# Splitting each expert tile's sixteen matmuls over two steps of the scan loop on TensorE

## What is computed

```python
u, v = split(x @ in_proj_w.T + in_proj_b)
delta = softplus(u @ delta_proj_w.T); A = -exp(a_log)
Bmat = (u @ b_proj_w.T + b_proj_b).reshape(Bsz, L, G, N)
u_conv = silu(causal_conv(u))
# scan over time, for 1024 channels x 16 states:
h = exp(delta * A) * h + (delta * u_conv) * B;  y = sum_n h * c
attn = y * silu(v)

shared_out = swiglu(fx @ w_shared_in) @ w_shared_out
hid = swiglu(fx @ w1_shared)
for e in range(8):
    routed_out += wdense[:, e:e+1] * (hid @ w2[e])      # wdense: top-2 gate weights
```

## Time and profile before

| | us |
|---|---|
| median of two runs | 5194.6 (5162.02 and 5227.19) |
| the profiled execution, its own time | 5190.78 |
| span of its slowest core (core 3), from first to last instruction | 5189.2 |
| spans of the eight cores | 5139.2 to 5189.2 |
| mean granted clock of PE, by core | 0.770 to 0.788 |

### The profile page before, as it was taken

The page is one execution under the profiler, slowest core; times in us unless marked ns, Lnnn a source line. Parts: engine busy times, 40 slices in busy tenths (PEclk is TensorE's granted clock), DMA queues, the critical chain, the costliest instruction groups (busy, mean ns, idle before and its releaser), DMA issues.

```text
span 5189.2 us, 45260 instructions; the slowest of 8 cores (5139.2 to 5189.2 us)
## 1 busy us (share of the span) xinstructions
PE 2806.7 (54%) x10240; PEld 1037.8 (20%) x10240; DVE 3187.6 (61%) x4304; ACT 1671.4 (32%) x2403; POOL 1746.5 (34%) x2319
## 2 busy tenths in 40 slices
PE   0025764556725765457645667258663577455673
PEld 0002221212202221122212222022221222121221
DVE  0014788268863789357872788527884478825886
ACT  0014521353213712255213622137121452225421
POOL 0002544045420634035340544206340264403543
PEclk9997886678857987588866888568775688667885
DMA  9961220212211221112212122012211122121220
GB/s 105 111 96 64 71 92 35 83 48 75 86 42 51 75 75 68 53 55 76 83 35 83 58 75 83 34 51 75 75 68 41 59 75 84 43 77 40 74 85 25
DMA packets 50961, 348.47 MB, mean 67 GB/s; under 512 B 6224, under 2 KB 6480, under 8 KB 16880
## 3 DMA queue, kind: packets, MB, share of 16 engines
q1 hardware_dynamic: 46144, 302.30, 16.7%
q0 software_dynamic: 1488, 34.88, 6.3%
q10 hardware_dynamic: 3072, 8.39, 0.5%
HBM read 363.66 MB, written 51.38 MB: 80 GB/s over the span
## 4 chain that ended last, share of the span: by engine, by line
DVE 30%; PE 25%; issue 16%; POOL 11%; ACT 7%; another core or an unknown queue 7%; DMA 3%; DVEq 1%; POOLq 0%; ACTq 0%; SPq 0%
DVE hsc L816 13%; POOL ysc L847 7%; DVE dBu L811 6%; PE pEG L929 6%; DVE hg L778 4%; DVE uc L718 3%; PE pAB L877 3%; PE pAB L480 3%; PE pFF L480 2%; PE pBCb L594 2%; DVE accb L576 1%; POOL acc L852 1%; POOL state L843 1%; PE pBCb L462 1%
## 5 line engine op out<-in xcount | busy, mean ns | idle before, releaser
L671 ACT ACTIVATE dA<-dlt,A_sb 128x512 f32<-128x512 bf16 x1024 | 737.0, 721 | 1946.9 <-DVE hsc L816 1943.0
L929 PE MATMUL pEG<-hg,ring 128*128 128x512 bf16 x4096 | 1041.2, 413 | 548.9 <-DVE hg L778 390.6
L816 DVE TENSOR_TENSOR_SCAN hsc<-dA,state,dBu 128x512 bf16<-128x512 f32 x768 | 1265.9, 1648 | 82.9 <-DVE dBu L811 3.7
L847 POOL TENSOR_TENSOR ysc<-hsc,ysc 128x512 f32<-128x512 bf16 x960 | 1129.5, 1177 | 0.8 <-issue 0.8
L811 DVE TENSOR_TENSOR dBu<-du,pBCb 128x512 bf16<-128x512 bf16 x1024 | 684.7, 669 | 441.8 <-PE pBCb L948 397.8
L843 POOL CAST state<-hsc 128x1 f32<-128x1 bf16 x1024 | 224.0, 219 | 1707.9 <-DVE hsc L816 1694.5
L929 PEld LDWEIGHTS pEG<-hg,ring 128*128 128x128 bf16 x4096 | 409.1, 104 | 1171.7 <-issue 865.9
L826 POOL TENSOR_TENSOR du<-du,dlt 128x512 bf16<-128x512 bf16 x64 | 73.6, 1149 | 1672.8 <-ACT du L656 1672.8
L948 PE MATMUL pBCb<-b_sb,csel_sb 32*128 32x512 bf16 x1024 | 392.1, 426 | 401.5 <-DVE dBu L811 360.6
L816 DVE TENSOR_TENSOR_SCAN hsc<-dA,dBu 128x512 bf16<-128x512 f32 x256 | 420.5, 1643 | 26.8 <-DVE dBu L811 0.5
L462 PE MATMUL pBCb<-ident,xnp 128*128 128x128 f32 x256 | 94.6, 446 | 581.8 <-DVE xnp L422 558.3
(11 more groups left out here) (94 smaller groups left out, 2980.4 us busy)
## 6 DMA issues: line engine op xcount, KB each, us to landing
ring<-wsbf SPq DMA_DIRECT2D x256, 1024.0 KB, 4.8
wsbf<-wstream POOLq DMA_DIRECT2D x8, 4096.0 KB, 184.3
x_tok<-x SPq DMA_DIRECT2D x8, 2048.0 KB, 8.9
out<-x_tok SPq DMA_DIRECT2D x8, 2048.0 KB, 7.5
csel_sb<-cselbf ACTq DMA_DIRECT2D x64, 128.0 KB, 2.3
cselbf<-csel POOLq DMA_DIRECT2D x1, 1024.0 KB, 336.8
wbp_sb<-wbp POOLq DMA_DIRECT2D x1, 256.0 KB, 335.7
selc_sb<-selc SPq DMA_DIRECT2D x1, 128.0 KB
```

The costliest lines, as they stand in the source:

```text
L671: sc.activation(dA[:, j % 2, 0:TC], dlt[:, gg, :], AF.Exp, scale=A_sb[:, gg, n:n + 1]).then_inc(S.sa_da, 1)
L816: v.tensor_tensor_scan(hsc[:, j % 2, 0:TC], dA[:, j % 2, 0:TC], dBu[:, j % 2, 0:TC], init, ALU.mult, ALU.add).then_inc(S.sv_sc, 1)
L847: ins = gp.tensor_tensor(ysc[:, gg % 2, :], hsc[:, j % 2, 0:TC], ysc[:, gg % 2, :], ALU.add)
L929: ins = t.matmul(pEG[:, m % 2, :], ring_piece(p_idx)[:, kc, :], hg[:, ii, kc, :], start=first, stop=(ii == 1 and kc == NK - 1))
```

## The change

Each expert tile is cut into its two halves of eight matmuls, `ii` = 0 and 1. The first keeps its step, 44 + 16 ep + 2 m, the second goes one step further. Start and stop flags of the accumulation are kept over the two halves, and the waits for `hg`, for `eadd` and for the gates stand ahead of the first half only. `SWF_AFTER` of a tile keeps the count after its second half, so DVE waits for the same thing as before. No instruction is added or removed, except that a bc matmul now stands in the middle of each accumulation group (into another bank).

```diff
@@ -73,7 +73,8 @@
         T_GAPS.append((_SO_GAPS[_i] + _h, ("so", _i, _h)))
 for _ep in range(4):
     for _m in range(8):
-        T_GAPS.append((44 + 2 * (8 * _ep + _m), ("exp", _ep, _m)))
+        for _ii in range(2):
+            T_GAPS.append((44 + 16 * _ep + 2 * _m + _ii, ("exp", _ep, _m, _ii)))
 T_INV = {}
 for _g, _item in T_GAPS:
     T_INV.setdefault(_g, []).append(_item)
@@ -108,8 +109,8 @@
     if item[0] == "so":
         return [56 + 2 * item[1] + item[2]]
     if item[0] == "exp":
-        ep, m = item[1], item[2]
-        return [64 + 16 * ep + 2 * m, 64 + 16 * ep + 2 * m + 1]
+        ep, m, ii = item[1], item[2], item[3]
+        return [64 + 16 * ep + 2 * m + ii]
     return []
 
 
@@ -121,7 +122,7 @@
         ps = _item_pieces(_item)
         MAIN_ORDER.extend(ps)
         _cnt += len(ps)
-        SWF_AFTER[_item] = _cnt
+        SWF_AFTER[_item[:3] if _item[0] == "exp" else _item] = _cnt
 assert _cnt == 128 and len(MAIN_ORDER) == 104
 STREAM_ORDER = list(range(24)) + MAIN_ORDER
 POS = {p: i for i, p in enumerate(STREAM_ORDER)}
@@ -911,28 +912,26 @@
                 t.matmul(pEG[:, e % 2, :], selc8_sb[0:8, e, :], wdf[0:8, :],
                          start=True, stop=True).then_inc(S.st_gb, 1)
             else:
-                ep, m = item[1], item[2]
+                ep, m, ii = item[1], item[2], item[3]
                 q = 8 * ep + m
-                if q == 0:
-                    t.wait_ge(S.sa_gb, C_SAGB * c + 7)
-                elif q == 1:
-                    t.wait_ge(S.sa_gb, C_SAGB * c + 8)
-                if m == 0:
-                    t.wait_ge(S.sv_hg, C_SVHG * c + ep + 1)
-                if q >= 2:
-                    t.wait_ge(S.sv_em, C_SVEM * c + q - 1)
-                first = True
-                for ii in range(2):
-                    p_idx = 64 + 16 * ep + 2 * m + ii
-                    wait_piece(t, c, p_idx)
-                    for kc in range(NK):
-                        ins = t.matmul(pEG[:, m % 2, :],
-                                       ring_piece(p_idx)[:, kc, :],
-                                       hg[:, ii, kc, :],
-                                       start=first,
-                                       stop=(ii == 1 and kc == NK - 1))
-                        first = False
-                    ins.then_inc(S.swf, 1)
+                if ii == 0:
+                    if q == 0:
+                        t.wait_ge(S.sa_gb, C_SAGB * c + 7)
+                    elif q == 1:
+                        t.wait_ge(S.sa_gb, C_SAGB * c + 8)
+                    if m == 0:
+                        t.wait_ge(S.sv_hg, C_SVHG * c + ep + 1)
+                    if q >= 2:
+                        t.wait_ge(S.sv_em, C_SVEM * c + q - 1)
+                p_idx = 64 + 16 * ep + 2 * m + ii
+                wait_piece(t, c, p_idx)
+                for kc in range(NK):
+                    ins = t.matmul(pEG[:, m % 2, :],
+                                   ring_piece(p_idx)[:, kc, :],
+                                   hg[:, ii, kc, :],
+                                   start=(ii == 0 and kc == 0),
+                                   stop=(ii == 1 and kc == NK - 1))
+                ins.then_inc(S.swf, 1)
 
         for j in range(128):
             for item in T_INV.get(j, []):
```

## The result

The changed kernel takes 5099.1 us (median of 11 runs, 5070.3 to 5132.2) against 5187.8 us before (10 runs, 5159.0 to 5227.2): ratio 0.9825, with a 95% interval of 0.9783 to 0.9867. That is 1.8% faster, by 89 us (by the interval 1.3 to 2.2%, so whether it is more than 2% stays open); the forecast was 5110. Ratios here compare only executions in which no die ran markedly longer at a lower granted clock than the other, while medians are over all executions. Its profiled execution took 5074.1 us.

A forecast was written before the change was run, and what follows sets the result against it. DVE's loop sets each chunk's end, so its waits for bc matmuls behind hg go fully into the time. 70 + 12 + 3 - 4 = 81 us off 5190.8 gives 5110 us; range 5068 to 5160.

The forecast's parts named there:

- The 32 places: DVE's dBu waits for the bc matmul behind hg, once per expert pair and chunk: 70 us gained, bounds 57 and 80.
- The limit of 2.35 us: Most one place can gain: second scan ends at B+2.85 instead of B+5.21, B being the even step's bc matmul start.
- the shorter scan: Second scan behind hg takes 1.28 us instead of 1.89 if it starts after POOL's ysc addition is through.
- the new wait: In front of the second dBu behind hg, up to 1.3 us, partly free because POOL's addition falls into it.
- Steps 68 to 70: Wait at j = 70 nearly goes, wait at 68 moves to 69: 12 us gained, bounds 6 and 30.
- The csel loads: At j = 80 and 96 csel leaves before the ring pull: 3 us gained over 16 places, bounds 0 and 8.
- The cost on PE: Split tiles cost PE 4.30 us per pair of steps against 4.10: 4 us lost in last chunks, bounds 0 and 10.
- more: Rival, 0.11: all 80 us of second halves, 30 at steps 68 to 70, 8 at csel loads; 118 us, 5072 us.
- Less: Rival, 0.10: scan behind the new wait not shorter, wait at 70 turns up at 71, csel gives nothing; 5135 us.
- 57 - 1: Gain in us of the rival of 5135 us; 57 is 1.78 x 32, the scan staying at 1.89 us.
- Nothing: Rival, 0.03: something other than the second half, such as selector or ring, holds the first bc matmul; 5190 us.
- Slower: Rival, 0.04: granted clock falls in the steady stretch, two slow step pairs in each of 32 groups; 5334 us.

The follow-up runs named there:

- the experiment without POOL: Kernel before and changed kernel, each without POOL's addition of the scan's result at steps 44, 60, 76 and 92: 5154.7 and 5157.7 us, one execution each.
- the first experiment: Changed kernel with only the first expert tile of each pair split, the other seven whole: 5147.8 us (4 runs, too far apart for a verdict).
- the csel experiment: Kernel before, with each group's csel load issued by ACT eight steps earlier: 5215.5 us in one execution.
- the version two steps later: Changed kernel with all split tiles and their eadd two steps later, hg unmoved: 5007.5 us, then 4935.6 us (ratio to before 0.957) in a second series.

## Why the prediction was right

The time, the sign and the range held: 5110 forecast, 5099 measured, range 5068 to 5160. By its own steps:

- **The 32 places, 70 us.** Measured 66.2 (360.3 to 294.1). The limit of 2.35 us, set by the second bc matmul that stays where it is, and the shorter scan are in the rows: the new wait, the 1.28 us, and the experiment without POOL. The part of the wait that costs nothing was measured as 10 of 13 us.
- **Why this could be kept.** The prediction took it as given that the tiles behind the first one don't take it back. Only the first experiment showed that this rests on a second split: with the second tile whole, 31.4 us come back. The step was right for the change as a whole, its reason was not written down.
- **Steps 68 to 70, 12 us.** From step 66 to 72 the windows of core 5 shorten by 10.8 us, 139.8 to 129.0 (counted from dBu to dBu in the trace); on core 3, with the lower clock before, by 23.7. The wait at j = 68 went to 69 and that at j = 70 vanished, as said.
- **The csel loads, 3 us.** Undersized. The waits at 80 and 96 gave 4.8 us (5.22 to 0.41), and another 5.4 us at steps 86 and 102 were not in the sum at all. They stood where a tile ran partly at 1.2 GHz behind an idle time of PE. After the change the half ahead of step 102 runs at a granted clock of 1.00 in seven of eight chunks; why the clock no longer falls there stays open (see the csel experiment), so these 5.4 us were won without having been foreseen.
- **The cost on PE, 4 us.** Not there at a mean granted clock of 0.787: outside the 32 places and step 69 no dBu of an odd step waits. At a lower clock there is one. In the profile with 0.72 to 0.73 (the changed kernel without POOL's additions) most pairs of steps still take DVE 5.15 us (dBu at 2441.08 and 2446.23), for where a dBu starts a tenth of a microsecond late, the scan behind it takes 1.68 in place of 1.89:

```profile
2441.08 0.67 DVE L812 TENSOR_TENSOR dBu<-du,pBCb 128x512 bf16<-128x512 bf16 x1
...
2443.26 0.69 DVE L812 TENSOR_TENSOR dBu<-du,pBCb 128x512 bf16<-128x512 bf16 x1
2444.05 1.68 DVE L817 TENSOR_TENSOR_SCAN hsc<-dA,state,dBu 128x512 bf16<-128x512 f32 x1
...
2446.23 0.67 DVE L812 TENSOR_TENSOR dBu<-du,pBCb 128x512 bf16<-128x512 bf16 x1
```

But the waits at odd steps outside the places and step 69 sum to 35.6 us there, and the stretch is 34.4 us longer than the changed kernel's 1768.7:

```profile
sum 1803.10, PE 1389.91 PEld 462.29 DVE 1532.15 ACT 398.40 POOL 738.87; mean PE 173.74 PEld 57.79 DVE 191.52 ACT 49.80 POOL 92.36
```

The kernel before loses less at a low clock: in the csel experiment its stretch is 1873 to 1875 us on cores 0 to 3 (0.735 to 0.739) and 1854 to 1857 on cores 4 to 7, 18 us. So the change is worth some 70 us in the stretch at such a clock, an estimate from these two profiles, and the prediction's 4 us are small for it.

Corrected, the sum is 66 + 11 + 10 - 0 = 87 us, against 89.7 in the stretch. The first two terms held by their mechanism. That 81 came so near is in part luck: 5 us too much in the first two terms stand against 11 too little in the last two.

By its own list of signs: the first dBu waits 4.0 us in the mean in place of the 3.8 forecast, the new wait is 0.07 to 1.00 us in the 32 places, and in the ten places where it is over 0.6 us the scan behind it takes 1.23 to 1.28.

The rivals: "more" needed all of the second halves and failed at the second bc matmul. "Less" had its one part, the scan, refuted, and the wait at 70 did not turn up at 71 (its 57 - 1 isn't broken down in the prediction). "Nothing" fell with the first row. "Slower" needs PE at 1.2 GHz in the steady stretch. It didn't come: the mean granted clock of core 5 in the eight windows of the stretch is 0.84 to 0.85 before and 0.85 to 0.86 after, and the splitting added no idle times: outside the waits for hg, PE's idle times over 0.05 us in the stretch of core 5 are 226 before (291 us) and 152 after (177 us). The effect that the Trainium skill tells of ("TensorE: Matmul & The Clock Gate", section "A second HAM failure mode: psum-queue depth-cycling") did not appear here. In a steady pair the eight matmuls after a bc matmul start 0.32 us behind it (2465.93 and 2466.25), and the next bc matmul follows at once.

## What to carry to other kernels

Where one engine's in-order queue carries short operations that another engine waits for, and long blocks of filler between them, the block's length is what the other engine waits for after each restart; cut the fillers to one step's size, all of them, since the first whole block behind takes back what the split one gave. Cutting is worth 1.8% here, but putting the blocked filler behind the operations that are already free (two steps later) is worth 4.3% with it and 3.3% without: ask first what stands behind the wait, then how long it is. And read what a new wait costs from the end of the next operation, not from the wait: here three quarters of it were free, since a neighbour's operation fell into it.

## What was not expected of the hardware

- The length of DVE's scan follows POOL's addition: in these rows it takes 1.08 us and the overlap, and not under about 1.28. Before, the scan from 2490.91 meets the addition, which ends at 2491.72, for 0.81 us: 1.89. After, from 2465.14, it meets it for 0.24: 1.32. So the wait of 0.47 us ahead of that dBu cost nothing. In the 32 places of the changed kernel the scan takes 1.70 to 1.72 us behind most waits of 0.07, 1.44 behind one of 0.34, and 1.23 to 1.28 from 0.53 on.
- After the waits for hg, 11.4 to 13.5 us of idle time, the first eight matmuls take 3.1 to 3.5 us to the next operation, at a granted clock of 0.50 to 0.57 (0.50 is 1.2 GHz), in all 32 places; with 7.2 to 7.8 us of idle time (the version two steps later) they take as long, 3.1 to 3.5 us.
- Behind idle times of 2.05 to 2.27 us one and the same tile, the one ahead of step 102, runs at a mean granted clock of 0.67 in some chunks and at 1.00 in others (5 and 3 of 8 before, 0 and 8 with only the first tile split).
